# A four-layer graph network on one core: Layer 2's exponentials in PSUM, with new order lists

## What is computed

```python
q, k, v = (proj(Wq, bq), proj(Wk, bk), proj(Wv, bv))
scores = jnp.einsum('bhqd,bhkd->bhqk', q, k) * SCALE
mask = (adj_matrix + bond_matrix)[:, None, :, :]
scores = scores * mask
attn = jax.nn.softmax(scores, axis=-1)
ctx = jnp.einsum('bhqk,bhkd->bhqd', attn, v)
```

## Time and profile before

| what | us |
|---|---|
| median of 3 runs | 962.69 |
| the runs | 962.51, 962.69, 967.75 |
| span of the profiled execution, first to last instruction | 966.0 |
| TensorE busy, of the span | 887.1 (92%) |
| VectorE, ScalarE, GpSimd busy | 742.3, 724.6, 670.3 |

### The profile page before, as it was taken

One profiled execution on the slowest core, in us unless ns is written; L12 is line 12 of the kernel. 1 busy time (PEld: TensorE's weight loads), 2 busy tenths in 40 slices (PEclk: granted clock), 3 DMA queues, 4 the chain that ended last, 5 costly groups with the idle time before them and its releaser, 6 DMA issues.

```text
span 966.0 us, 34322 instructions
## 1 busy us (share of the span) xinstructions
PE 887.1 (92%) x12124; PEld 761.5 (79%) x12124; DVE 742.3 (77%) x2292; ACT 724.6 (75%) x1740; POOL 670.3 (69%) x1005
## 2 busy tenths in 40 slices
...
GB/s 207 20 21 83 111 100 65 119 111 106 112 123 121 116 116 102 103 112 109 106 109 110 122 123 117 114 106 99 111 119 103 104 115 116 109 97 116 97 48 22
DMA packets 194573, 99.46 MB, mean 103 GB/s; under 512 B 112866, under 2 KB 194276, under 8 KB 194532
## 3 DMA queue, kind: packets, MB, share of 16 engines
...
## 4 chain that ended last, share of the span: by engine, by line
PE 53%; ACT 11%; POOL 10%; DVE 10%; issue 9%; DMA 5%; SPq 1%; POOLq 0%; DVEq 0%; ACTq 0%
PE bank L537 12%; PE bank L539 12%; PE bank L538 12%; POOL rFl L1375 3%; PE bank L562 3%; ACT r L886 3%; PE bank L754 2%; PE bank L815 2%; DMA k_by_head<-kst 2%; DMA Ks<-k_by_head 2%; PE bank L650 1%; ACT x L846 1%; PE bank L682 1%; ACT rFh L826 1%; POOL rsC L1391 1%
## 5 line engine op out<-in xcount | busy, mean ns | idle before, releaser
L1375 POOL TENSOR_TENSOR rFl<-r,rFh 128x512 f16<-128x512 f32 x64 | 74.2, 1160 | 81.1 <-ACT rFh L826 81.1
L537 PE MATMUL bank<-z1h,W 128*128 128x256 f16 x256 | 71.9, 281 | 6.3 <-DVE z1l L1025 6.3
L538 PE MATMUL bank<-z1l,W 128*128 128x256 f16 x256 | 71.8, 281 | 0.0
L537 PE MATMUL bank<-W,rFh 128*128 128x256 f16 x256 | 71.8, 280 | 0.0
L539 PE MATMUL bank<-z1h,W 128*128 128x256 f16 x256 | 71.7, 280 | 0.0
L539 PE MATMUL bank<-W,rFl 128*128 128x256 f16 x256 | 71.7, 280 | 0.0
L538 PE MATMUL bank<-W,rFh 128*128 128x256 f16 x256 | 71.7, 280 | 0.0
L1476 POOL TENSOR_TENSOR late<-late,Smx 128x512 f32<-128x512 f32 x64 | 66.8, 1043 | 1.3 <-DVE Smx L1282 1.0
L1375 POOL TENSOR_TENSOR y0l<-y,y0h 128x512 f16<-128x512 f32 x32 | 37.3, 1166 | 42.3 <-ACT y0h L826 42.3
L870 ACT ACTIVATE Pf<-bank,Dinv 128x128 f32<-128x128 f32 x64 | 20.0, 363 | 49.7 <-DVE Dinv L1167 49.7
L886 ACT ACTIVATE r<-bank,b1c 128x256 f32<-128x256 f32 x128 | 50.1, 471 | 4.8 <-PE bank L539 4.8
...
## 6 DMA issues: line engine op xcount, KB each, us to landing
Qs<-q_by_head SPq DMA_DIRECT2D x96, 128.0 KB, 2.7
Ks<-k_by_head SPq DMA_DIRECT2D x96, 128.0 KB, 3.2
Vbd<-vst SPq DMA_DIRECT2D x128, 66.0 KB, 2.1
xin<-x SPq DMA_DIRECT2D x32, 256.0 KB, 2.8
q_by_head<-qst SPq DMA_DIRECT2D x32, 256.0 KB, 2.5
k_by_head<-kst SPq DMA_DIRECT2D x32, 256.0 KB, 2.1
out<-late SPq DMA_DIRECT2D x32, 256.0 KB, 2.9
...
```

What stands on the lines that cost most here:

```text
L537: pe.matmul(o, sh, mh, start=start, stop=False, skip_group_check=True)
L538: pe.matmul(o, sh, ml, start=False, stop=False, skip_group_check=True)
L1375: return pool.tensor_tensor(dst, a, b, ALU.subtract)
```

## The change

The tile `E` goes away. The exponentials of tile t are written into the PSUM bank that held the scores of tile t (bD0 or bD1, all 512 columns), and the cast and the subtraction read them there. The bank is therefore free only when the low half has been made: the x2 transpose of the next group waits for `e_lo` in place of `s_masked`. All order lists are new. Number and kind of the instructions are otherwise the same.

```diff
-        E = sb("E", [P, TILES, HEADS, NODES])
+        def exps(t):
+            return (bD0, bD1)[t][:].rearrange("p (h k) -> p h k", h=HEADS)
...
                 pe.wait_ge(ev("xC"), at.n())
                 if at.earlier(1):
-                    pe.wait_ge(ev("s_masked"), at.tile(1, -1))
+                    pe.wait_ge(ev("e_lo"), at.tile(1, -1))
                 turn(bD0, x2).then_inc(ev("x2_turned"), 1)
...
-                    act.activation(E[:, t], Ssb[:, t], ACT.Exp, scale=SOFT2).then_inc(ev("exp"), 1)
+                    act.activation(exps(t), Ssb[:, t], ACT.Exp, scale=SOFT2).then_inc(ev("exp"), 1)
...
-                    cast(Ehl[:, t, 0], E[:, t]).then_inc(ev("e_hi"), 1)
+                    cast(Ehl[:, t, 0], exps(t)).then_inc(ev("e_hi"), 1)
...
-                    dve.tensor_tensor(Ehl[:, t, 1], E[:, t], Ehl[:, t, 0], ALU.subtract).then_inc(ev("e_lo"), 1)
+                    dve.tensor_tensor(Ehl[:, t, 1], exps(t), Ehl[:, t, 0], ALU.subtract).then_inc(ev("e_lo"), 1)
...
-ORDER_PE = [3, 2, 1, 5, 2, 4, 4, 2, 0, 3, 1, 0, 2, 0, 5, 4, 0, 0, 5, 3, 1, 3, 4, 5, 1, 2, 5, 5, 2, 0, 1, 0, 4]
-ORDER_SP = [3, 0, 5, 3, 4, 3, 0, 3, 0, 2, 3, 2, 2]
+ORDER_PE = [1, 2, 3, 5, 3, 1, 2, 0, 5, 4, 4, 0, 2, 5, 0, 4, 3, 3, 5, 0, 0, 2, 4, 1, 5, 1, 5, 0, 1, 2, 0, 2, 4]
+ORDER_SP = [3, 3, 0, 4, 0, 3, 3, 0, 3, 5, 2, 2, 2]
...
-ORDER_ACT = [0, 4, 3, 2, 1, 0, 0, 3, 5, 0, 5, 2, 5, 1, 4, 0, 0, 0, 0, 1, 2, 0, 4, 5, 0, 3, 2, 4, 3, 4, 1, 4, 2, 3, 3, 4, 5]
-ORDER_DVE = [0, 0, 0, 2, 0, 2, 1, 0, 0, 0, 2, 2, 0, 0, 3, 4, 4, 1, 4, 0, 1, 4, 1, 2, 0, 5, 3, 5, 4, 5, 3, 3, 5, 3, 5, 1, 3, 4, 5, 2, 3, 3, 1, 5, 5, 0, 0, 5, 2, 0, 1, 3, 1, 4]
-ORDER_POOL = [0, 1, 0, 0, 1, 0, 3, 4, 1, 1, 1, 2, 1, 2, 0, 5, 3, 0, 0, 0, 4, 4, 3, 4, 5, 5, 5, 0, 0]
+ORDER_ACT = [4, 1, 3, 5, 2, 5, 3, 0, 0, 5, 0, 0, 4, 4, 5, 4, 1, 0, 3, 0, 0, 3, 0, 0, 1, 0, 2, 3, 4, 1, 3, 2, 2, 4, 2, 4, 5]
+ORDER_DVE = [0, 1, 0, 2, 0, 0, 0, 3, 2, 0, 1, 0, 0, 5, 0, 3, 3, 4, 4, 4, 5, 2, 0, 4, 1, 5, 1, 5, 5, 0, 3, 3, 2, 5, 4, 3, 3, 2, 3, 4, 1, 1, 3, 0, 0, 0, 5, 2, 1, 5, 5, 1, 2, 4]
+ORDER_POOL = [0, 0, 1, 1, 0, 0, 4, 3, 1, 5, 1, 1, 3, 3, 0, 0, 0, 2, 0, 2, 1, 4, 4, 0, 4, 5, 5, 0, 5]
...
```

More of the change, by code:

```diff
@@ L44 @@
 SQUARED = "CF"
-ORDER_PE = [3, 2, 1, 5, 2, 4, 4, 2, 0, 3, 1, 0, 2, 0, 5, 4, 0, 0, 5, 3, 1, 3, 4, 5, 1, 2, 5, 5, 2, 0, 1, 0, 4]
-ORDER_SP = [3, 0, 5, 3, 4, 3, 0, 3, 0, 2, 3, 2, 2]
-HEAD_SP = [[0, 0, 0], [0, 0, 0], [0, 0, 0, 2, 2, 2], [3, 3, 3, 0, 0, 3, 2, 3, 2, 2, 0], [3, 3, 0, 0, 0, 3, 4, 2, 3, 2, 2, 3], [3, 3, 0, 5, 0, 3, 0, 3, 3, 2, 4, 2, 2]]
-TAIL_SP = [[3, 3, 3, 3, 4, 2, 3, 2, 2, 5], [3, 3, 4, 5, 3, 3, 2, 3, 2, 2], [3, 3, 3, 4, 3, 3, 5], [5, 4], [5]]
-ORDER_ACT = [0, 4, 3, 2, 1, 0, 0, 3, 5, 0, 5, 2, 5, 1, 4, 0, 0, 0, 0, 1, 2, 0, 4, 5, 0, 3, 2, 4, 3, 4, 1, 4, 2, 3, 3, 4, 5]
@@ L57 @@
-HEAD_POOL = [[0, 0, 0, 0, 6, 0, 0, 0, 0, 0, 0], [0, 0, 0, 1, 1, 0, 1, 1, 1, 0, 1, 0, 0, 0, 6, 0, 0], [0, 0, 0, 1, 1, 0, 1, 1, 1, 2, 2, 6, 1, 6, 6, 0, 0, 0, 0, 0, 0], [0, 0, 0, 1, 1, 3, 0, 1, 1, 1, 2, 2, 1, 3, 0, 3, 0, 0, 0, 0, 0], [0, 0, 1, 0, 1, 3, 4, 1, 0, 1, 2, 1, 2, 4, 4, 3, 4, 1, 0, 0, 0, 0, 3, 0, 0], [1, 3, 0, 0, 0, 0, 1, 4, 5, 1, 1, 1, 3, 2, 2, 4, 4, 3, 4, 1, 0, 0, 0, 0, 5, 0, 5, 5, 0]]
-TAIL_PE = [[3, 2, 4, 5, 1, 4, 5, 2, 3, 2, 4, 5, 1, 2, 3, 5, 3, 4, 5, 1, 2, 5, 2, 1, 4, 1], [4, 3, 2, 5, 4, 3, 5, 2, 4, 2, 5, 2, 4, 5, 3, 3, 5, 2, 5, 2, 4], [3, 5, 3, 4, 5, 4, 5, 4, 5, 4, 5, 5, 3, 3, 4], [5, 5, 4, 4, 4, 5, 4, 5, 5, 5, 4], [5, 5, 5, 5, 5, 5]]
@@ L61 @@
-TAIL_POOL = [[1, 1, 3, 4, 5, 1, 1, 1, 3, 1, 2, 2, 3, 4, 4, 4, 5, 5, 5], [4, 3, 5, 2, 2, 4, 4, 3, 3, 4, 5, 5, 5], [4, 5, 4, 4, 3, 4, 3, 5, 3, 5, 5], [4, 5, 4, 4, 4, 5, 5, 5], [5, 5, 5, 5]]
+ORDER_PE = [1, 2, 3, 5, 3, 1, 2, 0, 5, 4, 4, 0, 2, 5, 0, 4, 3, 3, 5, 0, 0, 2, 4, 1, 5, 1, 5, 0, 1, 2, 0, 2, 4]
+ORDER_SP = [3, 3, 0, 4, 0, 3, 3, 0, 3, 5, 2, 2, 2]
+HEAD_SP = [[0, 0, 0], [0, 0, 0], [0, 0, 0, 2, 2, 2], [3, 3, 0, 3, 3, 3, 0, 0, 2, 2, 2], [3, 4, 3, 0, 3, 0, 0, 3, 3, 2, 2, 2], [3, 3, 4, 5, 3, 3, 0, 0, 0, 2, 3, 2, 2]]
@@ new lines @@
+TAIL_SP = [[3, 4, 5, 3, 3, 3, 3, 2, 2, 2], [3, 4, 3, 3, 3, 5, 3, 2, 2, 2], [3, 4, 3, 5, 3, 3, 3], [4, 5], [5]]
+ORDER_ACT = [4, 1, 3, 5, 2, 5, 3, 0, 0, 5, 0, 0, 4, 4, 5, 4, 1, 0, 3, 0, 0, 3, 0, 0, 1, 0, 2, 3, 4, 1, 3, 2, 2, 4, 2, 4, 5]
+ORDER_DVE = [0, 1, 0, 2, 0, 0, 0, 3, 2, 0, 1, 0, 0, 5, 0, 3, 3, 4, 4, 4, 5, 2, 0, 4, 1, 5, 1, 5, 5, 0, 3, 3, 2, 5, 4, 3, 3, 2, 3, 4, 1, 1, 3, 0, 0, 0, 5, 2, 1, 5, 5, 1, 2, 4]
+ORDER_POOL = [0, 0, 1, 1, 0, 0, 4, 3, 1, 5, 1, 1, 3, 3, 0, 0, 0, 2, 0, 2, 1, 4, 4, 0, 4, 5, 5, 0, 5]
@@ new lines @@
+HEAD_PE = [[0, 0, 6, 0, 6, 0, 0, 6, 0, 0], [1, 0, 0, 1, 0, 0, 0, 1, 6, 1, 1, 0, 0], [2, 1, 2, 2, 0, 2, 0, 1, 0, 0, 0, 2, 1, 1, 2, 1, 0, 0], [3, 1, 3, 2, 0, 2, 0, 2, 1, 0, 2, 3, 3, 0, 0, 1, 2, 0, 1, 2, 1, 0], [4, 1, 3, 2, 4, 3, 0, 2, 4, 2, 1, 0, 4, 0, 2, 3, 3, 0, 1, 0, 1, 1, 4, 2, 0, 0, 2], [5, 4, 2, 3, 1, 2, 5, 2, 4, 5, 3, 1, 4, 5, 0, 2, 3, 3, 0, 5, 5, 0, 4, 1, 0, 0, 1, 2, 1, 0, 2, 4, 0]]
+HEAD_ACT = [[0, 0, 6, 0, 0, 6, 0, 0, 0, 0, 0, 0], [6, 0, 6, 6, 6, 1, 0, 0, 0, 1, 0, 0, 0, 1, 0, 0, 0, 1, 6], [0, 2, 1, 0, 0, 2, 0, 1, 0, 2, 0, 0, 1, 0, 0, 2, 0, 1, 2], [6, 3, 6, 6, 0, 3, 1, 2, 0, 0, 0, 2, 0, 3, 0, 3, 0, 0, 0, 3, 0, 3, 1, 2, 1, 2, 1, 6, 2], [1, 3, 0, 4, 3, 2, 4, 0, 0, 4, 4, 0, 4, 1, 2, 4, 0, 1, 3, 0, 0, 3, 0, 0, 1, 0, 3, 3, 2, 4, 2, 2], [5, 5, 3, 2, 0, 5, 1, 4, 3, 4, 5, 0, 4, 0, 4, 3, 1, 0, 2, 3, 1, 3, 4, 0, 0, 0, 0, 0, 1, 0, 3, 2, 4, 2, 2, 4, 5]]
```

11 lines of the change are left out of this document (6 added, 5 removed).

## The result

The changed kernel takes 1030.66 us (median of four runs, 1030.30 to 1032.61) against 965.22 us for the kernel before (962.51 to 968.20): 1.0709 times the time, 95% interval 1.0671 to 1.0747. The profiled execution took 1030.45 us, its span is 1028.6 against 966.0.

What follows compares the result with a forecast made beforehand. TensorE was taken to bound the kernel at 26.48 us a step; the new lists' seven-link loop across engines makes 28.8, and 26 x 2.32 = 60 us on 962.69 gives 1023 us, range 974 to 1050.

Steps and rivals of the forecast that it cites:

- link 7: ScalarE from norm of B to norm of C without a gap, then handover to the x2 transpose: 9.97 us.
- links 3 and 4: GpSimd's veG, rsG, rsc, nbG: 2.23 us; then ScalarE's norm of G, gw, y0h, K's high half: 3.16 us.
- Links 1, 2 and 6: x2 transpose to x2Fl, 1.28 us; VectorE's x2Fl to statistics of G, 2.17; GpSimd's SAs, rsB, nbB, 2.41.
- Rival M: Experiments' rival: another chain of nearly equal length stands right behind, so shortening a link gains little; no chance given.
- link 6: GpSimd from takeover through SAs, rsB and nbB to ScalarE's norm of B: 2.41 us.
- The PSUM part: Exponentials, casts and subtractions using a PSUM bank: ScalarE saves 0.16 us a step, VectorE's subtraction unchanged.
- The new wait: TensorE's x2 transpose waits for the exponentials' second low half, forecast level with the norm of C at 28.8 us.
- A: Rival: a shorter loop through Q's low half, VectorE's queue and TensorE, 27.2 us a step, 982 to 1005 us; chance 0.20.
- B: Rival: TensorE stays the bound, the step stays 26.48 us, the time 955 to 971 us; chance 0.13.
- C: Rival: faster, TensorE's wait for SAs, 0.38 us a step, goes, giving 953 us; chance 0.06.
- D: Rival: worse, idling TensorE gets less clock (0.93), 29.3 to 29.8 us a step, 1036 to 1050 us; chance 0.09.
- E: Rival: PSUM part does nothing visible, lists alone make the result; moves the forecast at most 4 us; inside its 0.52.

Runs made afterwards that it cites:

- run 1: All the changed kernel's new order lists on the kernel before, exponentials still in E in SBUF and the old s_masked wait: 1036.49 us, ratio 1.0748.
- run 7: Changed kernel plus one 512-wide ScalarE copy a step, between the casts of r: 1049.44 us, ratio 1.0927.
- run 8: Changed kernel plus one 512-wide ScalarE copy a step, ahead of xgFh where ScalarE then idles: 1036.45 us, ratio 1.0791.
- run 11: Changed kernel plus two TensorE transposes a step ahead of w_sum: 1033.72 us, ratio 1.0758.
- run 5: Changed kernel with y0h and K's high half ahead of gw on ScalarE, K's low half ahead of HBh on VectorE: 1024.40 us, ratio 1.0647.
- run 6: Changed kernel with nbG ahead of rsc on GpSimd and K's low half ahead of HBh on VectorE: 1025.68 us, ratio 1.0669.
- run 2: Changed kernel with ScalarE's norm of B moved behind both relus: 1047.91 us, ratio 1.0885.
- run 3: Changed kernel with y0h and K's high half moved ahead of gw on ScalarE: 1031.86 us, ratio 1.0696.
- run 9: Kernel before plus one 512-wide ScalarE copy a step, between the casts of r: 979.35 us, ratio 1.0189.

## Why the prediction was right, and where it was off

The forecast of 1023 us was 8 us short: 3 are the step (28.92 for 28.8), 2.5 the median of the kernel before, which is 965.22 with four runs and was 962.69 with three, and the rest what lies between span and median, less the 0.6 of head and tail.

**The loop of the lists** was right and is shown: run 1 has it without the PSUM part, run 7 lengthens link 7 by what it adds, runs 8 and 11 add work beside it for nothing, runs 5 and 6 shorten links 3 and 4 by what their rows say. Links 1, 2 and 6 rest on the rows alone. Rival M was right in two places: in run 2 a second way out of SAs, in run 3 VectorE's own queue with the stretched HBh came next at once. By links, forecast against measured: 1.28 and 1.32; 2.17 and 2.28; 2.23 and 2.26; 3.16 and 3.16; 7.60 and 529.99 - 522.42 = 7.57; link 6, 2.41 and 531.97 - 529.99 = 1.98; link 7 with its handover, 9.97 and 513.40 - 503.01 = 10.39. The sum, 28.96 for this turn, stands against 28.82.

**Two terms were mis-sized**, by 0.43 and 0.42 us in opposite directions, so that the sum comes within 0.1 us of the step is in part luck. In link 6 nbB takes 0.50 us in place of 0.94. In link 7 the norm of C does not follow ScalarE's queue at once: Ehl is through at 512.07, a cast's 0.48 after its start, but rsC on GpSimd ends only at 512.33, and the transpose starts 0.12 us after the norm, not 0.05. From the second rFl (508.20), which ScalarE's cast of r releases, GpSimd runs without a gap over 0.1 us to rsC, so the loop leaves ScalarE there, and the last part of link 7 that the prediction gave to ScalarE is GpSimd's.

**The PSUM part** was taken as 0.16 us a step and is 0.05 (run 1). The rows of one instruction came about as forecast (cast 601 ns, had 640; exponential 600, was 634), but from start to start the exponential still takes 0.52 us (504.73 to 505.25). Only the casts gain, 0.04 each start to start (506.48 to 506.96 where those from SBUF take 0.52), and the second stands where GpSimd's rsC decides. VectorE's subtraction takes 687 ns from the bank, 702 from SBUF before: the row was right against the Trainium skill's table (VectorE: DVE Perf Modes, "The TRN2 errata"), by which it would have been longer. What the prediction had no term for is the subtraction beside GpSimd, 1036 ns from SBUF in run 1, off the loop.

**The new wait** cost nothing of its own: the second low half ends at 512.35 + 0.68 = 513.03, the norm of C at 512.37 + 0.91 = 513.28, and TensorE waits for the norm. That is near the level the prediction gave. K's DMAs land in 2.5 us and do not set the end, as forecast; TensorE waits for K once between 200 and 900 us (1.2 us), where the prediction had 0.4 in every step. Head and tail came out at 63.2 - 62.6, under 1 us, in these two executions.

**What the prediction said one would see**: the step and the 0.60 us casts are there, and ScalarE waits for nbB, by 0.19 us. TensorE's windows read 56.7 of 60 busy, not 54, and of the three waits of 0.5 us only that for y3l is so long; those of the products for x1Fl and the norm of C are 0.2. TensorE's busy time rose for the same products, from 59.82 / 60 x 26.48 = 26.4 us a step to 56.67 / 60 x 28.92 = 27.3, so busy time may hide part of the idling.

**The rivals.** A and B fell with the step. C's wait did not go: TensorE still waits 0.3 us for SAs, since SAs ends at 530.56, after the scores (530.29). D did not occur: with TensorE 56.67 of 60 us busy the clock read 1.00, the 2.4 GHz level. E is the finding of run 1 for the step, inside the forecast.

**The step that was wrong in its reason** is the first one, that TensorE alone bounds the kernel before and covers the others: run 9 shows ScalarE's stretch up to x1Fh level with it. The forecast did not suffer, as the change moved all the orders.

No version here beats the kernel before. Run 5, the best of the PSUM versions, is at 1.0647. Whether other lists would bring the PSUM version to 26.5 us a step stays open. So does what the bank costs under the old lists, which was not run: the prediction put the new wait at 8 us there, and run 1 weighs the bank under the new lists alone.
